# The order of GpSimd's steps before the expert stage, and a place of its own for the last context block

## The reference, cut to what matters

```python
hn = layernorm(x); n = rmsnorm(hn) * norm_w
pool = concat([n, ctx], axis=1)                 # own rows and context rows
attn = softmax(mask(n @ q_w.T @ (pool @ k_w.T).T * scale))
alpha = sigmoid(hn @ gate_w.T + gate_b)
x = x + (1 - alpha) * hn + alpha * (attn @ pool)
```

```python
y = layernorm(x).reshape(2048, 256)
for e in range(8):
    g = y[tok[e]]                                # gather 512 rows
    o = gelu(g @ W1[e] + b1[e]) @ W2[e] + b2[e]
    out[tok[e]] += o * combine_weights[tok[e], e]
x = x + out
```

## Time and profile before

| | before |
|---|---|
| median of three runs | 281.68 us (281.52 to 282.61) |
| the profiled execution's own time | 283.24 us |
| its span, first to last instruction | 281.5 us |
| PE busy | 268.5 us (95%) |
| DVE, ACT, POOL busy | 221.5, 179.6, 160.8 us |
| attention stage and first rows, until ScalarE's first copy for expert 0 (L710) | 88.2 us |
| mean granted TensorE clock | 0.997 |

### The profile page before, as it was taken

One profiled execution on the slowest core, in us unless ns is written; L12 is line 12 of the kernel. 1 busy time (PEld: TensorE's weight loads), 2 busy tenths in 40 slices (PEclk: granted clock), 3 DMA queues, 4 the chain that ended last, 5 costly groups with the idle time before them and its releaser, 6 DMA issues.

```text
span 281.5 us, 5498 instructions
## 1 busy us (share of the span) xinstructions
PE 268.5 (95%) x1698; PEld 238.6 (85%) x1698; DVE 221.5 (79%) x526; ACT 179.6 (64%) x341; POOL 160.8 (57%) x153
## 2 busy tenths in 40 slices
PE   6999999997879999999999999999999999999992
PEld 2789899997756888999899899999989999899992
DVE  1788999898586579988797797887889879787652
ACT  2488899885474856656658576666655856663540
POOL 4284866653851883556456665645645666514655
PEclk9999999999999999999999999999999999999998
DMA  6992257477245854455544643456445462110121
GB/s 215 356 261 82 76 149 202 137 226 260 94 117 167 289 189 147 151 196 156 144 148 142 187 165 127 151 137 207 150 135 150 155 184 79 57 36 26 40 77 67
DMA packets 30293, 42.45 MB, mean 151 GB/s; under 512 B 5251, under 2 KB 24015, under 8 KB 30148
## 3 DMA queue, kind: packets, MB, share of 16 engines
q1 hardware_dynamic: 25392, 30.00, 33.6%
q0 software_dynamic: 4608, 12.24, 15.3%
q10 hardware_dynamic: 276, 0.00, 0.1%
HBM read 33.54 MB, written 9.24 MB: 152 GB/s over the span
## 4 chain that ended last, share of the span: by engine, by line
PE 73%; DVE 7%; DMA 7%; issue 4%; POOL 4%; ACT 3%; SPq 1%; DVEq 0%; POOLq 0%; ACTq 0%
PE bank L1154 20%; PE bank L1156 20%; PE bank L1155 20%; DMA x_all<-token_rows,idx_all 2%; PE bank L1292 2%; PE bank L1197 2%; PE bank L1241 2%; DMA setup_or_probs<-in_L_xattn_k_w_dram 2%; DMA token_rows<-qT 1%; DMA token_rows<-xn 1%; PE bank L1138 1%; PE bank L1315 1%; PE bank L1312 1%; PE bank L1311 1%; POOL x_all L531 1%
## 5 line engine op out<-in xcount | busy, mean ns | idle before, releaser
L729 ACT ACTIVATE keysT<-bank,biasT 128x512 f32<-128x512 f32 x63 | 43.4, 690 | 66.1 <-PE bank L1156 55.4
L544 POOL DMA_INDIRECT out_dram<-h,sidx x32 | 38.6, 1207 | 38.0 <-DVE h L1044 30.9
L535 POOL DMA_INDIRECT x_all<-out_dram,idx_all x32 | 38.5, 1202 | 23.8 <-DMA out_dram<-h,sidx 16.3
L1154 PE MATMUL bank<-x_hi,w_hi 128*128 128x512 f32 (+1 forms) x114 | 45.2, 397 | 0.0
L1156 PE MATMUL bank<-x_hi,w_lo 128*128 128x512 f32 (+1 forms) x114 | 44.2, 388 | 0.0
L1155 PE MATMUL bank<-x_lo,w_hi 128*128 128x512 f32 (+1 forms) x114 | 44.1, 387 | 0.0
L531 POOL DMA_INDIRECT x_all<-token_rows,idx_all x28 | 29.6, 1057 | 22.6 <-DVE factor L1095 8.8
L1051 DVE SCALAR_TENSOR_TENSOR junk<-idx_rows,idx_f,normed 128x512 bf16<-128x512 bf16 (+1 forms) x32 | 38.8, 1212 | 3.6 <-POOL normed L555 3.6
L1077 DVE TENSOR_TENSOR w_lo<-w_raw,w_hi 128x512 fp32r<-128x512 f32 x56 | 38.4, 685 | 0.0
L1156 PE MATMUL bank<-w_hi,g_lo 128*128 128x256 f32 x128 | 36.3, 283 | 0.0
L1155 PE MATMUL bank<-w_lo,g_hi 128*128 128x256 f32 x128 | 36.2, 283 | 0.0
(11 more groups left out here) (168 smaller groups left out, 715.3 us busy)
## 6 DMA issues: line engine op xcount, KB each, us to landing
w_raw<-in_L_ffn_W_dram SPq DMA_DIRECT2D x32, 512.0 KB
hn_cnat<-in_ctx_dram SPq DMA_DIRECT2D x8, 256.0 KB, 2.8
idx_rows<-in_L_ffn_top_idx_dram SPq DMA_DIRECT2D x8, 256.0 KB
out_dram<-x SPq DMA_DIRECT2D x8, 256.0 KB, 4.9
token_rows<-xn SPq DMA_DIRECT2D x7, 256.0 KB, 2.2
hn_cnat<-in_L_ffn_b_dram SPq DMA_DIRECT2D x1, 1024.0 KB, 7.8
x_all<-in_x_dram SPq DMA_DIRECT2D x3, 256.0 KB, 4.6
x_all<-in_x_dram SPq DMA_DIRECT2D x1, 768.0 KB, 8.3
```

Of the source, the lines that this page charges most:

```text
L535: g.indirect_dma_start(accg[:, t, :], None, flat, list_of(e, t)).then_inc(acc_in[t], 16)
L544: g.indirect_dma_start(flat, idx(sidx[:, t:t + 1].bitcast(U32), 0), newrow[:, t, :], None, bounds_check=N - 1, oob_is_err=False).then_inc( ...
L729: a.activation(g32[:, f % NG, :], ps_up[f % 2][:, :], ACT.Gelu_apprx_tanh, bias=bias)
L1154: t_.matmul(dst, lhs_hi, rhs_hi, start=first, stop=False)
```

## The change

It has five parts.

1. POOL: the gather of tile 0 moves from behind `x_plus_h` of pair 6 to the end of POOL's turn for pair 6, behind `normed`, the weights' low part and `rstd` of pair 5.
2. POOL: in the turn of pair 7 the gathers of tiles 1, 2 and 3 are issued together, behind `x_plus_h`; before, tile 3's came behind `rstd` of pair 6. So `rstd` of pair 6 is now behind three gathers.
3. SP and TensorE: the context of pair 7 goes to a place of its own, `cnat_last`, in columns 1056 to 1567 of `x_all`. SP issues its load in the round r = 3, right behind the load for pair 6, after a wait for `x_plus_h` of pair 3; before, it was issued in round r = 4 after the values product of pair 5.
4. VectorE: the shift of pair 6 moves from the middle of `last_pair_mixed(1)` to right behind `last_pair_mixed(0)`.
5. TensorE: the last four one-hot products (low part of pair 7) go bank by bank, so the first bank is finished after two of them; before, it was finished after three.

```diff
+        cnat_last = x_all[:, NT * ROW:NT * ROW + 2 * H].rearrange("p (b h) -> p b h", b=2)
@@ SP
-                if r + 3 < NPAIR:
+                if r + 3 < LAST:
                     sp.wait_ge(pv_mm, r + 2)
                     load_ctx(r + 3)
+                if r == EARLY_PAIRS - 2:
+                    sp.wait_ge(xh_rdy, r + 1)
+                    sp.dma_start(cnat_last, c_v[:, 2 * LAST:2 * LAST + 2, :]).then_inc(c_in_s[LAST % 2], 16)
@@ POOL, attention(p, s)
-                if p == LAST - 1:
-                    gather_first_rows(range(1))
                 if is_last(p):
-                    gather_first_rows(range(1, NT - 1))
+                    gather_first_rows(range(1, NT))
@@
                     rstd(p - 1, 1 - s)
-                if is_last(p):
-                    gather_first_rows(range(NT - 1, NT))
+                if p == LAST - 1:
+                    gather_first_rows(range(1))
@@ DVE, last_pair_mixed(b)
-                if b == 1:
-                    shift(NPAIR - 2, 1 - last_s)
@@ DVE, after the last pair
             last_pair_mixed(0)
+            shift(NPAIR - 2, 1 - last_s)
             last_pair_variance(0)
@@ PE, context_transposes and values product
+                rows = cnat_last if is_last(p) else cnat[:, s, :, :]
-                        last = t_.transpose(ps_cT[:, k, b, :], cnat[:, s, b, k * P:(k + 1) * P], ident[:, :])
+                        last = t_.transpose(ps_cT[:, k, b, :], rows[:, b, k * P:(k + 1) * P], ident[:, :])
@@
-                        values = normed if j == 0 else cnat
+                        context = cnat_last if is_last(p) else cnat[:, s, :, :]
+                        values = normed[:, s, :, :] if j == 0 else context
@@ PE, the last one-hot products
-            for b in range(2):
-                pe.wait_ge(late_lo_rdy, 3 + b)
-                late_rows(2, b, late_lo, last_one=b == 1)
+            for k in range(KH):
+                for b in range(2):
+                    pe.wait_ge(late_lo_rdy, 3 + b)
+                    last = t_.matmul(ps_xT[k][:, :], late_lo[2][:, b, k * P:(k + 1) * P], onehot[:, 4 + b, :],
+                                     start=False, stop=(b == 1))
+                last.then_inc(xT_mm, 1)
```

More of the change, by code:

```diff
@@ L1239, in attention @@
                     for j in range(2):
-                        values = normed if j == 0 else cnat
+                        context = cnat_last if is_last(p) else cnat[:, s, :, :]
+                        values = normed[:, s, :, :] if j == 0 else context
                         last = t_.matmul(ps_pv_last[b] if is_last(p) else ps_pv[:, b, :], probsT[:, b, j, :],
-                                         values[:, s, b, :], start=(j == 0), stop=(j == 1))
+                                         values[:, b, :], start=(j == 0), stop=(j == 1))
                     if is_last(p) and b == 0:
@@ L1259, in early_rows, with late_rows @@
                                   start=False, stop=False)
-            def late_rows(n, b, part, first=False, last_one=False):
+            def late_rows(n, b, part, first=False):
                 pe.wait_ge(onehot_rdy, 2 * n + b + 1)
                 for k in range(KH):
[L1265 to L1268, removed]
+                    t_.matmul(ps_xT[k][:, :], part[n][:, b, k * P:(k + 1) * P], onehot[:, 2 * n + b, :],
+                              start=first, stop=False)
             each_pair(pe, attention)
```

## The result

The changed kernel takes 278.04 us (median of four runs, 277.88 to 279.16), the kernel before 281.64 (281.52 to 282.61). The ratio is 0.986, with an interval of 0.983 to 0.989: 3.6 us faster, where 2.7 were forecast.

What follows compares the result with a forecast made beforehand. TensorE was taken to set the pace from 100.92 us on; the later of rows (98.2) and TensorE (97.3) counts, 2.7 us sooner, so 281.68 - 2.7 = 279.0 us. The range was 278.2 to 280.6.

Steps and rivals of the forecast that it cites:

- Tile 0: Gather ahead of the last pair's values product on TensorE: lands at 73.3 to 75.3, wanted by 75.06, costing nothing.
- no stall at the shift: VectorE's shift after last_pair_mixed(0), at 78.56: the power of pair 6 ends in time, stall 0, bounds 0 to 0.7.
- TensorE's way: TensorE through expert 0's late products to expert 1's transposes: 3.4 us sooner, there at 97.3.
- the forecast's term is 2.13: High part of pair 5 on TensorE starts 2.13 us sooner, at 73.61, and the last pair's first VectorE step follows.
- The rows' way: Last rows' stores on SP, then POOL's gathers for expert 1: rows there at 98.2, 2.7 us sooner.
- The landing of 3.98: Store of the last rows before expert 1's gathers: takes 3.98 us as before and moves along with its start.
- the last gather with its 6.45 us: Last of POOL's four gathers for expert 1: its 6.45 us landing carried over, ending at 98.2.
- 0.9 us of waiting at the transposes: TensorE reaches expert 1's transposes at 97.3 and waits 0.9 us for the rows.
- rival B: Last gather for expert 1 benefits fully from sooner biases, TensorE's way binds: 3.4 us gained, 278.3; chance 0.08.
- the sooner biases: The 1 MB of biases beside expert 1's gathers moves 3.4 us sooner, letting the last gather land sooner.
- those 180.6 us are not touched: Stretch from expert 1's transposes at 100.92 to the end at 281.5, paced by TensorE: 180.6 us, unchanged.

Runs made afterwards that it cites:

- parts 1 to 3 alone: Kernel before with POOL's new gather order and the last context's own place, without the sooner shift and new product order: 279.60 us, ratio 0.991.
- the stores held back: Changed kernel with SP's stores of the normalised rows of pairs 5 and 6 held until VectorE's last step: 280.55 us, ratio 0.992 to before.
- without part 4: Changed kernel with the shift of pair 6 back inside last_pair_mixed(1): 280.44 us, ratio 0.994 to before.
- either part alone: Two kernels from the one before: POOL's gather order alone, 282.50 us, ratio 1.000; the last context's own place alone, 282.57 us, ratio 1.001.
- the held-back gathers: Changed kernel with POOL's 1.8 us memset put ahead of the gathers for expert 1: 277.81 us, ratio 0.983 to before.
- the context alone: Kernel before with only the last context's own place and earlier load added: 282.57 us, ratio 1.001.

## Why the forecast was too small

**Step by step, aligned.** Part 1: VectorE's shift was forecast at 70.32 and came at 70.55 (the small `var_eps` took 0.90 instead of 0.17 beside POOL). Part 3: the wait of 1.41 is gone; the high part of pair 5 was forecast at 73.61 and came at 73.31. Tile 0 was no hindrance. The first step of the last pair was forecast at 77.16 and came at 77.08. Part 2: the power of pair 6 was to end at 77.9 to 78.4 and ended at 77.90; no stall at the shift, 78.40 against 78.56. Part 4: the last shift came at 82.59, 0.3 later than forecast, since the last power took 0.96 instead of 0.56. The last half of the rows left at 83.2 (forecast 83.0). ScalarE's copy for expert 0 came at 84.82 (forecast 84.8), so TensorE's way was right: 97.3 forecast, 97.21 measured. For parts 1 to 3 alone the forecast's term is 2.13, and the trace of that kernel gives 2.3.

**The step that failed** is "The rows' way": "The landing of 3.98 and the gathers up to 100.87 move with it: 98.2." Both durations were taken over from the trace of before. The last half left when it should, but landed in 2.3 us instead of 3.98, so the gathers started 4.1 sooner where 2.7 were forecast. The landing of the earlier trace rows is not the store's own time. SP sends a batch: pair 6's rows, a list, `x2`, two halves. From the start of pair 6's store, the second of L404 (L400 before, at 83.7), to the first gather it took 6.8 us before, 6.6 in the change, 6.7 with the stores held back, 6.7 without part 4, 6.7 with parts 1 to 3, 6.7 and 6.8 with either part alone, and 6.6 to 7.0 in all thirteen profiles in which POOL waits for it. The last half left 1.9 to 2.0 us into it in seven of them and 2.9 to 3.4 in six, so its landing was 3.8 to 4.0 in the former and 2.3 to 2.9 in the latter. In the kernel before the DMA engines are at work through that batch (windows, the last but one column is the DMA share):

```profile
84.00:85.00 1.00, 1.00 (x6) 0.72 (x5) 0.64 (x2) 1.00 (x3) 0.38 (x1) 1.00 0.99 333
85.00:86.00 1.00, 1.00 (x6) 0.82 (x5) 0.96 (x5) 0.81 (x2) 0.00 (x0) 1.00 0.94 266
86.00:87.00 1.00, 1.00 (x6) 0.82 (x5) 0.27 (x1) 0.00 (x0) 0.00 (x0) 1.00 0.68 165
87.00:88.00 1.00, 1.00 (x6) 0.77 (x5) 0.00 (x0) 0.00 (x0) 0.00 (x0) 1.00 1.05 346
88.00:89.00 1.00, 0.47 (x3) 0.11 (x1) 0.19 (x1) 0.81 (x2) 0.00 (x0) 1.00 0.56 195
```

From 89 us on they are at rest (0.02), and the last half has landed at 89.7. So the start of pair 6's store is the term to follow: with the forecast's own SP times (first store at 80.0, the second 0.5 behind) and the 6.8 of before the gather would have been put at 87.3 instead of 87.8, and with the store as it came, aligned 78.4 + 1.4 = 79.8, at 86.6; measured 86.4. The other 0.7 is for the most part a slip on the stores: the forecast held the first, pair 5's, for the rows of pair 6, for which only the second waits in the code. It left at 79.3 aligned, and the second right when its rows were there. Which transfer of the batch costs what was not tried. The Trainium skill, DMA: Bandwidth & Descriptors, "Queues, rings and completion order", says that a transfer's completion is written only after every earlier write of the same DMA engine; the trace agrees in that the last half's landing follows what left ahead of it.

The other half of the step was the last gather with its 6.45 us. That it isn't fixed is shown by the held-back gathers, which landed within 5.1 and cost nothing. So the forecast's 0.9 us of waiting at the transposes never came, and TensorE's way was binding. That is the outcome of rival B, with a chance of 0.08; its reason, the sooner biases, was not tried apart from the sooner gathers. Its price of 3.4 leaves out the 0.21 us that TensorE waited before: 100.92 - 97.3 is 3.6, and the measured gain up to the transposes was 3.7.

**The smaller miss:** "those 180.6 us are not touched". They became 180.3. VectorE waits 3.6 us for POOL's table in the kernel before, 3.0 in the change and 5.3 with the stores held back. In the fourteen profiles the stretch behind the transposes is 180.2 to 180.3 us in the seven where this wait is 3.0 or less, 180.5 to 180.8 in the six where it is 3.6, and 181.7 in the one where it is 5.3. So the two go together; no run changes the wait alone. 3.7 and 0.3 are the 4.0.

**The forecast's own unease** about the profiled run was well placed but not followed up: it said that the run stood 1.56 above the median and carried the 2.7 over. That was right for the sum, since the excess lies in the first twelve microseconds.

## What to carry to other kernels

Before a landing time from a trace is moved along with its transfer, look at what left the same queue in the microseconds ahead of it: in a batch that leaves within a few microseconds the last landing can follow the batch's start (here pair 6's store) and not its own, and then moving the start is what counts. Where two ways of nearly equal length meet, give each its own forecast and ask which durations in it are borrowed from a collision that the change dissolves. Two edits that are each worth nothing by the medians can be worth 2 us together, if each removes one of two waits that cover each other; and a wait of TensorE that grows from 0.3 to 1.85 us can cost nearly its length once more through the clock, so look at the granted clock of each run before an edit is called worthless.

## What the runs showed of the hardware

- The granted clock fell to 0.50 after TensorE stood 1.85 and 2.05 us among short groups (two profiles), and stayed at 1.00 after 1.52 in the kernel before and after 1.36 without part 4. The length of the wait alone doesn't decide it: with the context alone TensorE stood 2.13 us and the clock of that profile stayed at 1.00 (below), while in six of that kernel's twelve executions the mean was 0.985 to 0.991.

```profile
74.00:75.00 1.00, 0.00 (x0) 0.00 (x0) 1.00 (x6) 0.97 (x2) 0.85 (x2) 1.00 1.05 372
```

- At the start the same four products took 2.08 us before and 1.13 in the change, after 0.8 us of idleness behind the warm-up in both; the changed kernel with its gathers held back, whose start is the same code, took 2.07 after 0.68. With what follows it is 1.4 us of the kernel's time.
- VectorE's mix with two operands in SBUF took 1.52 us instead of 0.69 while POOL's `x_plus_h` ran (70.58 to 71.88). The Trainium skill, SBUF — State Buffer, "SBUF: two separate sides", has such an operation and one of GpSimd's exclude each other for the whole instruction; the trace agrees. POOL's gather in turn took 1.72 beside the mix and the step behind it, and 0.94 to 1.23 in the change's three in a row.
- Even the smallest operations take longer beside one of the other engine: 0.90 instead of 0.17 for `var_eps` on VectorE (67.37, while POOL's low part of the weights ran from 66.97 to 68.24), 0.96 instead of 0.56 for the last power on POOL (80.23, while VectorE's L1006 ran from 80.08 to 80.77).
